# Tokenizer of a one-core vision kernel: the second half of the scores in front of the means, and two engine orders changed with it

## The reference

```
x = features.reshape(b, c, h, 4, w, 4)
reduce_feats = x.mean((3, 5))                      # one token per 4x4 patch: 256 tokens an image
q  = LN(reduce_feats) @ Wq.T                       # 8 heads of 8
kv = LN(every pixel)  @ Wkv.T                      # k and v of all 4096 pixels
attn  = softmax over the 16 pixels of a patch (q * scale . k)
aggre = sum over the 16 pixels (attn * v)
h = reduce_feats + aggre @ proj_w.T + proj_b
```

## Time and profile before

| | |
|---|---|
| median of 3 runs | 650.3 us (649.91 to 650.62) |
| span of the profiled execution, first to last instruction | 644.3 us |
| the profiled execution's own device time | not given; the median of the runs stands for it, 6.0 us above the span |
| tokenizer in the profile | up to about 320 us, the tail of it overlapped with the scan |
| PE busy over the span | 600.7 us (93%) |
| DVE busy | 538.7 us (84%) |
| ACT busy | 476.6 us (74%) |
| POOL busy | 473.0 us (73%) |

### The profile page before, as it was taken

One profiled execution on the slowest core, in us unless ns is written; L12 is line 12 of the kernel. 1 busy time (PEld: TensorE's weight loads), 2 busy tenths in 40 slices (PEclk: granted clock), 3 DMA queues, 4 the chain that ended last, 5 costly groups with the idle time before them and its releaser, 6 DMA issues.

```text
span 644.3 us, 16919 instructions
## 1 busy us (share of the span) xinstructions
PE 600.7 (93%) x5362; PEld 325.9 (51%) x5362; DVE 538.7 (84%) x1027; ACT 476.6 (74%) x942; POOL 473.0 (73%) x453
## 2 busy tenths in 40 slices
PE   3999999999999999998779989998689999999995
PEld 1222333333333333332345656665378889898894
DVE  4589999999999999998747888998887888888882
ACT  3888777777778777873358878887568878888882
POOL 5957988889988898755850456666787877777777
PEclk9999999999999999999869999999989999999998
DMA  8432233333322233000029492111131222222210
GB/s 287 156 145 97 112 131 132 132 131 131 116 76 88 115 132 132 20 2 14 1 78 200 98 211 54 39 37 38 56 102 53 68 66 72 60 53 67 57 40 1
DMA packets 49755, 58.04 MB, mean 90 GB/s; under 512 B 32476, under 2 KB 45252, under 8 KB 47448
## 3 DMA queue, kind: packets, MB, share of 16 engines
q1 hardware_dynamic: 44280, 48.12, 25.2%
q0 software_dynamic: 5120, 6.99, 3.5%
q10 hardware_dynamic: 288, 2.10, 0.9%
HBM read 50.13 MB, written 10.28 MB: 94 GB/s over the span
## 4 chain that ended last, share of the span: by engine, by line
PE 39%; DVE 6%; issue 2%; POOL 1%; DMA 1%; ACT 1%; POOLq 0%; DVEq 0%; ACTq 0%
PE s_logits L2078 13%; PE s_delta L2051 3%; PE s_proj L2051 3%; DVE x_px L1484 2%; PE s_ln L2085 2%; PE s_proj L1663 2%; PE s_logits L1757 2%; PE s_delta L1685 2%; PE s_ln L2056 2%; PE s_proj L2056 2%; PE s_proj L1673 1%; PE s_proj L1698 1%; PE s_proj L1697 1%; PE s_ln L1644 1%; PE s_ln L1735 1%
## 5 line engine op out<-in xcount | busy, mean ns | idle before, releaser
L2103 POOL DMA_INDIRECT out<-orow,m_rows x96 | 119.1, 1241 | 34.6 <-issue 19.1
L815 PE MATMUL s_proj<-x_px,w_kv 64*64 64x512 f32 x256 | 129.9, 599 | 0.0
L812 PE MATMUL s_proj<-x_px,w_kv 64*64 64x512 f32 x256 | 129.1, 596 | 0.4 <-DVE vec L235 0.3
L1205 POOL DMA_INDIRECT rows_by_group<-r_pay,r_slot_i x64 | 68.5, 1070 | 44.9 <-DVE r_slot_i L1534 8.4
L486 POOL TENSOR_TENSOR half_px<-x_px 128x1024 f32<-128x1024 f32 x30 | 71.4, 2380 | 32.9 <-DMA x_px<-in_x 32.9
L507 POOL TENSOR_TENSOR pre<-va 128x1024 f32<-128x1024 f32 x32 | 76.2, 2380 | 22.5 <-DVE va L608 20.7
L1947 DVE TENSOR_TENSOR m_xs<-m_rows,m_path_w 128x768 f32<-128x768 f32 x96 | 91.3, 951 | 1.1 <-PE s_proj L2056 0.7
L592 DVE TENSOR_TENSOR qk<-s_proj,q 128x512 f32<-128x512 f32 x128 | 85.5, 679 | 7.4 <-PE s_proj L815 5.1
L2078 PE MATMUL s_logits<-m_xsT,m_w_cur 128*64 128x128 f32 x1152 | 83.3, 275 | 0.0
L608 DVE TENSOR_TENSOR va<-b_a,v_sb 128x1024 f32<-128x1024 f32 x62 | 75.6, 1220 | 7.5 <-PE b_a L837 7.5
L308 ACT ACTIVATE x_sq<-x_px 128x1024 f32<-128x1024 f32 x64 | 67.1, 1048 | 19.2 <-PE b_x L872 19.2
(11 more groups left out here) (320 smaller groups left out, 1781.1 us busy)
## 6 DMA issues: line engine op xcount, KB each, us to landing
x_px<-in_x SPq DMA_DIRECT2D x15, 2048.0 KB, 7.9
m_rows<-rows_by_group SPq DMA_DIRECT2D x96, 72.0 KB, 1.9
wt<-in_w2T SPq DMA_DIRECT2D x8, 512.0 KB
rows_by_group<-rows_by_group SPq DMA_DIRECT2D x1, 2286.0 KB, 9.6
x_px<-in_x ACTq DMA_DIRECT2D x2, 1024.0 KB, 6.4
out<-orow,m_rows POOLq DMA_INDIRECT x96, 2.7
rows_by_group<-r_pay,r_slot_i POOLq DMA_INDIRECT x64
wt<-in_w2T SPq DMA_DIRECT2D x2, 256.0 KB
```

Source lines behind the costliest of these rows:

```text
L812: mm(b_k[i][LO, :], w_kv[LO, 0, LO], px(t, j, LO), start=True, stop=True)
L815: mm(b_k[i][HI, :], w_kv[HI, 0, HI], px(t, j, HI), start=True, stop=True).then_inc(done["kv_product"], 1)
L1205: g.indirect_dma_start(rows_d, bass.IndirectOffsetOnAxis(ap=slot_i[:, c % 2, k:k + 1], axis=0), pay[:, c % 2, k, :], None).then_inc(scatte ...
L2103: nc.gpsimd.indirect_dma_start(out_d, bass.IndirectOffsetOnAxis(ap=rows[:, i, ID0:ID0 + 1].bitcast(I32), axis=0), orow[:, i, :], None, bou ...
```

## The change

On TensorE `scores(t-2, 1)` is issued in iteration t between `kv(t-1, 1)` and `mean(t-1)`, for the scores of tiles 0 to 14; before, it was issued as `scores(t-1, 1)` one iteration earlier, between `kv(t, 0)` and `q_mm(t)`. It moves back past `q_mm`, `spread(t-2, 2)` and `kv(t-1, 1)`. The scores of tile 15 keep their place. On VectorE, in iterations up to 16, `q_scale` and `va_mul(t-3, 2)` and the first two `qk_mul` of the next tile come ahead of `scale_scores`; `scale_scores`, `scores_max` and `shift_scores` then follow each other directly, and `sum_exps` and `scale_exps` too, with `qk_mul(t-1, 2)` now ahead of `sum_exps`. On ScalarE `softmax_exp` goes behind `copy_v(t-1, 1)` and `kv_mean(t-1)`. No instruction is added or taken out, and no wait is changed.

```diff
@@ ScalarE
             square(t - 1, 2)
-            softmax_exp(t - 2)
             copy_v(t - 1, 1)
             kv_mean(t - 1)
+            softmax_exp(t - 2)
             copy_v(t - 1, 2)
@@ VectorE
             va_mul(t - 3, 1)
-            scale_scores(t - 2)
-            q_scale(t - 1)
-            scores_max(t - 2)
-            va_mul(t - 3, 2)
+            if t <= TILES:
+                q_scale(t - 1)
+                va_mul(t - 3, 2)
+                qk_mul(t - 1, 0)
+                qk_mul(t - 1, 1)
+                scale_scores(t - 2)
+                scores_max(t - 2)
+            else:
+                scale_scores(t - 2)
+                scores_max(t - 2)
+                va_mul(t - 3, 2)
             shift_scores(t - 2)
-            qk_mul(t - 1, 0)
-            qk_mul(t - 1, 1)
+            qk_mul(t - 1, 2)
             sum_exps(t - 2)
-            qk_mul(t - 1, 2)
             scale_exps(t - 2)
             va_mul(t - 3, 3)
@@ TensorE
             kv(t - 1, 1)
+            if t < TILES + 1:
+                scores(t - 2, 1)
             mean(t - 1)
...
             kv(t, 0)
-            scores(t - 1, 1)
+            if t >= TILES:
+                scores(t - 1, 1)
             q_mm(t)
             spread(t - 2, 2)
```

## The result

The changed kernel takes 659.23 us (658.68 to 660.22, 4 runs) against 650.46 us (649.91 to 651.64, 4 runs) for the kernel before beside it: a ratio of 1.0154, 95% interval 1.0129 to 1.0179. The direction was forecast, the size was not: +8.8 us instead of +2.4, outside the range that ended at 655.0.

A forecast was written before the change was run, and what follows sets the result against it. TensorE's gapless stream was taken as the bound. Iteration 2's 1.17, tile 1's 0.18 and 13 x 0.08 for the steady periods sum to 2.4 us, so 650.3 becomes 652.7 us; range for 8 in 10: 649.0 to 655.0.

The forecast's parts named there:

- The saving on TensorE: From the end of kv(t, 0) to chunk 2, two changes of shape go: 0.30 us saved a period, block 2.71 us.
- TensorE: the q product at 154.55 ..., scores' second half at about 156.8: Steady period on TensorE: the q product follows kv(t, 0) directly, 1.08 us earlier, and the scores' second half comes later.
- The last wait of the softmax is the one on the bank of the scores: The next tile's first half of scores waits for weigh, with only 0.40 us in hand before the change.
- The chain: VectorE, from chunk 2's multiplication to the start of weigh: 4.19 us instead of 3.47, with the sum now behind that multiplication.
- the handover: From the end of weigh on VectorE to TensorE's start on the scores: 0.05 us.
- The forecast stand of 0.38: TensorE waits 0.38 us for weigh ahead of the next scores in steady periods, so a period changes by +0.08 us.
- Dependent steps of VectorE: Softmax steps that need the one in front take 0.72 to 0.73 us against 0.60; if free, the chain is 0.12 shorter.
- Iteration 2: First softmax: ScalarE's copy_v of chunk 2 comes late, TensorE stands 1.9 us ahead of chunk 4; +1.17 us once.
- (a): Rival: chain some 0.1 to 0.2 us shorter and iteration 2's loss balanced; +0.5, 650.8 us; chance 0.2.
- (c): Rival: TensorE's stand in iteration 2 lowers the clock; +4.1, 654.4 us; chance 0.08.
- (b): Rival: weigh meets the scores, 14 periods each give 0.30; -3.0, 647.3 us, or 645.8 with iteration 2's loss hidden; chance 0.17.
- VectorE has 1.5 us of air: In steady periods VectorE has 1.5 us to spare beside a gapless TensorE; used as support for (b).

The follow-up runs named there:

- e6: The e5 kernel with spread(t-2,1) ahead of kv(t-1,7) on TensorE and va_mul(t-3,0) and va_mul(t-3,1) one multiplication earlier on VectorE; ratio 0.9928 to the kernel before.
- e9: The changed kernel with only the spread order of e6; 657.08 us, ratio 1.0133 to the kernel before.
- e10: The kernel of e6 run once more on another set of executions; 644.74 us, ratio 0.9937 to the kernel before.
- e3: The changed kernel with finish put in front of va_mul(t-3,3) up to iteration 16; 658.48 us, ratio 1.0144 to the kernel before.
- e5: The e4 kernel with iteration 2 in the old order on all three engines; ratio 0.9949 to the kernel before.
- e4: The changed kernel with va_mul(t-3,3) put behind weigh(t-2) up to iteration 16; 648.59 us, ratio 1.0000 to the kernel before.

## Why the prediction was wrong

Two waits of TensorE were put at nothing, and a third, the only one in the sum, is hidden behind one of them.

**The saving on TensorE** was right where it was sized: the block takes 2.72 us (2.71), and with all waits met e6 saves 0.39 a period. But in the changed kernel only 0.07 of it arrives: from the last pass of `kv(t, 0)` to chunk 2 it is 149.05 - 143.36 = 5.69, against 5.76 before. The first failed step is "TensorE: the q product at 154.55 ..., scores' second half at about 156.8". The scores used to lie between `kv(t, 0)` and the q product, and gave `va_mul(t-3,1)` the time to empty `b_a`. I moved everything behind them up by their length and did not ask what they had covered. `va_mul(.., 1)` was to end at 155.15 by my own rows, the q product at 154.98. e9 shows it: with this wait met, the period is 0.29 shorter.

**"The last wait of the softmax is the one on the bank of the scores"** is the second failed step, and the one that sank the size. The chain was followed through `va_mul(.., 3)` and `finish` to `weigh`, but `finish` was only counted as time on the way; that `square_sum` waits for it, one instruction ahead of the scores, was not looked up. The chain itself was right: `scale_exps`, `va_mul(.., 3)` and `finish` lie where they were worked out, and from chunk 2's multiplication to the start of `weigh` it is 154.41 - 150.20 = 4.21 (4.19). Put to the wait that was missed, it gives the stand: chunk 2 to its multiplication 1.15, 3.08 to `finish`, 0.41 for it and 0.14 for the handover are 4.78, against 4.05 of TensorE's work. So a period costs -0.30 + 0.24 + 0.73 = +0.67 (measured 0.66), instead of -0.30 + 0.38. By e9 and e10 both the saving and the first wait are a little larger, -0.36 and +0.29, with the same sum. That the sign came out right is partly luck: in the steady periods TensorE stands for other work than the forecast said.

**`weigh` and the scores.** The forecast stand of 0.38 isn't in the steady periods, because `square_sum` has stood before. It shows in iteration 3, which has no `finish` (TensorE in order of time, changed kernel):

```profile
61.46 1.06 PE L852 MATMUL b_s<-qk,sel 128*32 128x512 f32 x8 [0.41 <-DVE a_sb L678]
```

and in every period of e3. By the starts the stand in iteration 3 is 0.60: `square_sum` starts at 59.14 and the scores 2.32 behind it instead of 1.72; the forecast had 0.48. It lies behind `square_sum` of iteration 3 (-0.06), so it is counted in the next distance: +1.28 is this 0.60 and the steady 0.66. A term that was too small is the handover: `weigh` ends at 61.32, 0.14 ahead of the scores, and behind `finish` it is 0.14 too; the 0.05 was taken from a spread, and the changed kernel's spread shows 0.06.

**Dependent steps of VectorE.** In the changed kernel's trace sum to scale is 151.53 - 150.81 = 0.72, and a step that doesn't need the one in front comes 0.61 behind it (150.20 to 150.81). It isn't the kind of instruction: the scale step alone gives 0.73 to the maximum that needs it, and 0.62 to `q_scale`, which doesn't (155.77 to 156.39 in the kernel before). The Trainium skill ("VectorE: DVE Perf Modes", section "The DRAIN you can't avoid") says that a semaphore between consecutive VectorE instructions costs nothing extra; as I applied it here, the trace does not agree.

**Iteration 2** was right: +1.14, forecast +1.17, and e5 takes it away again (14.68). Its picture was partly wrong: the stand of 1.9 us ahead of chunk 4 is two, ahead of chunk 1 and of chunk 4, as TensorE's rows of the changed kernel show, each released by a copy of ScalarE:

```profile
33.98 0.61 PE L817 MATMUL s_proj<-x_px,w_kv 64*64 64x512 f32 x1 [0.61 <-ACT v_sb L400]
...
40.49 0.61 PE L817 MATMUL s_proj<-x_px,w_kv 64*64 64x512 f32 x1 [0.83 <-ACT v_sb L400]
```

The first of them is again a wait that the scores had covered: they used to stand ahead of chunk 1 there.

**The rivals.** (a) needed a chain 0.1 to 0.2 shorter than forecast; it is 4.21 against 4.19. (c), the lowered clock, did not come: the granted clock is 1.00 from 42 to 47 us, right behind iteration 2, and in the periods behind. (b), the other side, needed the way from chunk 2 to the scores to fit. In e4 it does, but the period falls by 0.10 and not by 0.30, and the time is that of the kernel before, not 3.0 us less: the wait of the spread, which (b) didn't have either, is still there. Only e6 and e10, with that wait and the loss of iteration 2 gone too, come near what (b) gave for that case: -3.9 us in e10 against -4.5. "VectorE has 1.5 us of air" was true and useful for e6, not for the change as it stood.

## What to carry to other kernels

Before a step is moved on an engine that is never idle, list for every instruction behind it all the semaphores it waits for, with the slack of each; what has been taken out was also the cover of someone else's work. Knowing a wait far down a chain isn't enough: an instruction ahead of it in the same queue may wait for an earlier link of the same chain, and then that wait decides. Where a change loses, look for the piece of the chain that nobody waits for (here one multiplication) before undoing it: with that, one spread moved and iteration 2 left as it was, the same idea gains 0.6 to 0.7%.

## What was not expected of the hardware

The start of the program varies from execution to execution: the first `square_sum` came at 22.58 us (e6, e9), 22.63 (before), 24.80 (e4) and 25.70 (after), and e10, the same kernel as e6, had it at 24.93. In the late ones TensorE's first passes of 512 columns lay 0.85 us apart instead of 0.43, up to about 20 us, although the granted clock is shown as 1.00 there. So up to 3 us between two traces can lie ahead of anything that the change touches, and a difference of spans should be read from the first common landmark on. Why the passes are slow there was not tried.
